# The third norm's rows split in row layout and turned by a transposing DMA in a macaron block

## What is computed

```python
x = x + 0.5 * ffn(layernorm(x), W_up, W_gate, W_down)
x = x + attention(layernorm(x), wq, wk, wv, wo)
x = x + 0.5 * ffn(layernorm(x), W_up, W_gate, W_down)
```

## Time and profile before

| | |
|---|---|
| median of 3 runs | 691.57 us (691.15 to 691.85) |
| the profiled execution | 692.43 us, span of its instructions 690.6 us |
| granted clock of TensorE, mean | 0.973 |
| busy, of the span | PE 603.4 us (87%), ACT 589.8 (85%), DVE 566.4 (82%), POOL 540.2 (78%) |
| DMA queue of the transposes and row copies | 68.1% of 16 engines' time |

### The profile page before, as it was taken

How to read it: one execution, slowest core, us unless ns; L and a number is a source line. 1 busy time by engine, 2 the same in 40 slices (tenths; PEclk the granted TensorE clock), 3 DMA queues, 4 the chain that set the end, 5 groups by cost and what they waited for, 6 DMA issues and landing times. The chain is left out here.

```text
span 690.6 us, 16960 instructions
## 1 busy us (share of the span) xinstructions
PE 603.4 (87%) x5961; PEld 474.4 (69%) x5961; DVE 566.4 (82%) x1457; ACT 589.8 (85%) x1179; POOL 540.2 (78%) x581
## 2 busy tenths in 40 slices
PE   1689996869999999999999999999988887969596
PEld 0366875647878787878787877778775655647374
DVE  3976688878998989898998989989987888777654
ACT  4255589989999999999999999999998999888742
POOL 2045868888989898989898989899897978785533
PEclk9999999999999999999999999999999999897889
DMA  8610419494979585877788696868688989795600
GB/s 328 193 39 1 93 32 196 76 203 77 177 101 189 96 174 110 154 138 129 141 129 164 116 161 119 166 98 169 108 173 144 163 142 182 126 178 92 131 1 32
DMA packets 311573, 90.44 MB, mean 131 GB/s; under 512 B 301760, under 2 KB 310208, under 8 KB 311488
## 3 DMA queue, kind: packets, MB, share of 16 engines
q1 hardware_dynamic: 310624, 87.06, 68.1%
q10 hardware_dynamic: 864, 2.29, 1.0%
HBM read 9.63 MB, written 4.19 MB: 20 GB/s over the span
## 5 line engine op out<-in xcount | busy, mean ns | idle before, releaser
L1614 POOL TENSOR_TENSOR hid_l<-hid,hid_h 128x512 f16<-128x512 f32 x128 | 149.1, 1165 | 91.9 <-ACT hid_h L842 91.8
L823 ACT ACTIVATE prob<-score_ps,exp_bias,exp_scale 128x128 f32<-128x128 f32 (+1 forms) x344 | 149.8, 516 | 9.6 <-DVE exp_bias L1251 8.7
L1609 POOL TENSOR_TENSOR prob_hl<-prob,prob_hl 128x768 f16<-128x768 f32 x86 | 141.9, 1650 | 12.5 <-ACT prob_hl L833 12.3
L416 PE MATMUL down_ps<-tern_down,hid_h 128*128 128x256 f16 x512 | 121.3, 277 | 20.6 <-POOL hid_l L1614 15.3
L416 PE MATMUL down_ps<-tern_down,hid_l 128*128 128x256 f16 x512 | 120.9, 276 | 0.0
L842 ACT ACTIVATE hid_h<-hid 128x512 f16<-128x512 f32 x128 | 81.8, 639 | 38.7 <-DVE hid L1286 38.1
L1277 DVE SCALAR_TENSOR_TENSOR silu_b<-tanh_b,up_ps 128x512 f32<-128x512 f32 x128 | 86.7, 677 | 15.9 <-ACT tanh_b L837 15.8
L837 ACT ACTIVATE tanh_b<-up_ps,tanh_scale 128x512 f32<-128x512 f32 x128 | 89.0, 695 | 12.5 <-PE up_ps L416 12.2
L1241 DVE TENSOR_REDUCE score_ps<-score_ps 128x2 f32<-128x512 f32 x128 | 88.4, 690 | 9.2 <-PE score_ps L426 9.1
L1286 DVE SCALAR_TENSOR_TENSOR hid<-silu_b,gate_ps 128x512 f32<-128x512 f32 x128 | 87.0, 680 | 2.6 <-DVE silu_b L1277 0.3
L424 PE MATMUL score_ps<-mask_b,ident_b 128*128 128x256 bf16 x256 | 69.4, 278 | 16.9 <-ACT prob L823 9.3
(11 more groups left out here) (111 smaller groups left out, 1506.1 us busy)
## 6 DMA issues: line engine op xcount, KB each, us to landing
xs<-x SPq DMA_DIRECT2D x16, 256.0 KB, 2.9
out<-xs SPq DMA_DIRECT2D x16, 256.0 KB, 3.3
raw_w<-prob_hl SPq DMA_TRANSPOSE x86, 3.8
raw_gate<-raw_gate SPq DMA_TRANSPOSE x42, 3.8
raw_up<-w_up_t ACTq DMA_DIRECT2D x1, 512.0 KB, 4.8
raw_gate<-w_gate_t ACTq DMA_DIRECT2D x1, 512.0 KB, 8.1
raw_up<-w_up_t SPq DMA_DIRECT2D x1, 512.0 KB, 9.9
raw_down<-w_down_t ACTq DMA_DIRECT2D x1, 512.0 KB, 10.2
```

What stands on the lines that cost most here:

```text
L416: mm = pe.matmul(dst, lhs, rhs, start=flags and n == 0, stop=n == len(pairs) - 1, skip_group_check=True)
L823: e = act.activation(prob[n % PT_BUFS][:, at + j * width:at + (j + 1) * width], score_ps[:, n % 2 if tile else 2, j * width:(j + 1) * widt ...
L1609: pool.tensor_tensor(prob_hl[n % PT_BUFS][:, 1, :], prob[n % PT_BUFS][:, :], prob_hl[n % PT_BUFS][:, 0, :], ALU.subtract).then_inc(prob_l_ ...
L1614: pool.tensor_tensor(hid_l[:, n % 2, :, :].rearrange("p m n -> p (m n)"), hid[:, n % 2, :], hid_h[:, n % 2, :, :].rearrange("p m n -> p (m ...
```

## The change

The third norm's rows are no longer turned by PE. The root that POOL makes now holds the factor 2^11 that was applied on the way out of PSUM. ACT writes the high part of `xhat` in row layout into a new tile `x_row3`, DVE writes the low part (xhat minus the high part) beside it, and SP issues one transposing DMA of 128x1024 f16 per batch from `x_row3` into the place from which `up` and `gate` read (`turn_xt`, semaphore `xt_turned`). `up` and `gate` of the second block wait for that transfer. The third norm leaves the count of the uses of `misc_ps`. `xt` now describes both layouts; for the third norm the parts lie tile by tile.

Besides, the order within the slots is another for PE, ACT, DVE and POOL, and some of the tables have other values. In the diff this is cut to its core:

```diff
@@ -72,18 +72,18 @@
-SUM_UP_AT = FIRST_FFN - 3
+SUM_UP_AT = FIRST_FFN - 2
...
-POWERS_AT = FIRST_FFN + 2
+POWERS_AT = FIRST_FFN + 1
...
-CASTS_AT = FIRST_FFN + 9
+CASTS_AT = FIRST_FFN + 8
...
-PE_TURN_AT = FIRST_FFN + 1
+PE_TURN_AT = FIRST_FFN + 2
@@ -114,20 +114,26 @@
-    1: {"stats": 4, "mean": 4, "var": 6, "power": 4, "shift": 3, "apply": 3},
-    2: {"stats": 3, "mean": 3, "var": 24, "power": 3, "shift": 2, "apply": 1},
-    3: {"stats": 2, "mean": 1, "var": 26, "power": 2, "shift": 2, "apply": 1},
+    1: {"stats": 5, "mean": 5, "var": 2, "power": 5, "shift": 4, "apply": 2, "turn": 1},
+    2: {"stats": 3, "mean": 3, "var": 11, "power": 3, "shift": 2, "apply": 1, "turn": 0},
+    3: {"stats": 2, "mean": 1, "var": 45, "power": 2, "shift": 2, "apply": 1, "turn": 2},
...
-ROPE_ADD = {-7: 0, -6: 1}
+ROPE_ADD = {-7: 0, -5: 1}
...
+TURNED = (3,)
+MISC_INDEX = {(what, b): n for n, (what, b) in enumerate(
+    (what, b) for _, _, what, b in MISC if not (what.startswith("norm") and int(what[-1]) in TURNED))}
@@ -239,12 +245,17 @@
         rstd = {k: sb(f"rstd{k}", [P, NT]) for k in (1, 2, 3)}
         shift = {k: sb(f"shift{k}", [P, NT]) for k in (1, 2, 3)}
         xhat = {k: sb(f"xhat{k}", [P, NT, E]) for k in (1, 2, 3)}
-        xt_hi = {k: sb(f"xt_hi{k}", [P, XT_BUFS[k], NC, SEQ], F16) for k in (1, 2)}
-        xt_lo = {k: sb(f"xt_lo{k}", [P, XT_BUFS[k], NC, SEQ], F16) for k in (1, 2)}
-
-
-        xt_3 = raw_up[:, :].bitcast(F16)[:, 0:2 * XT_BUFS[3] * NC * SEQ].rearrange("p (a b c n) -> p a b c n", a=2, c=NC, n=SEQ)
-        xt_hi[3], xt_lo[3] = xt_3[:, 0, :, :, :], xt_3[:, 1, :, :, :]
+        x_row = {k: sb(f"x_row{k}", [P, NT, 2, E], F16) for k in TURNED}
+        xt_all = {k: sb(f"xt{k}", [P, XT_BUFS[k] * 2 * W], F16)[:, :] for k in (1, 2)}
+        xt_all[3] = raw_up[:, :].bitcast(F16)[:, 0:XT_BUFS[3] * 2 * W]
+
+        def xt(k, b):
+
+            rows = xt_all[k][:, b % XT_BUFS[k] * 2 * W:(b % XT_BUFS[k] + 1) * 2 * W]
+            if k in TURNED:
+                return rows.rearrange("p (n a c q) -> p a c n q", a=2, c=NC, q=P)
+            return rows.rearrange("p (a c n q) -> p a c n q", a=2, c=NC, q=P)
+
 
         tanh_b = sb("tanh_b", [P, 2, 512])
         silu_b = sb("silu_b", [P, 512])
@@ -318,6 +329,7 @@
         shift_done = {k: sem(f"shift_done{k}") for k in (1, 2, 3)}
         xhat_done = {k: sem(f"xhat_done{k}") for k in (1, 2, 3)}
         xt_hi_done = {k: sem(f"xt_hi_done{k}") for k in (1, 2, 3)}
+        xt_lo_done, xt_turned = ({k: sem(f"{what}{k}") for k in TURNED} for what in ("xt_lo_done", "xt_turned"))
         tanh_done, silu_done, hid_done = sem("tanh_done"), sem("silu_done"), sem("hid_done")
...
@@ -381,6 +393,16 @@
                 sp.dma_start_transpose(k_pad[:, b % 2, :, cols],
                                        k_row[:, tile, :, :].rearrange("p h c -> p (h c)")).then_inc(stk_loaded[tile], 16)
 
+            def turn_xt(k, b):
+
+                if k in TURNED:
+                    if b >= XT_BUFS[k]:
+                        sp.wait_ge(up_done, ROUNDS * added(1 + k // 2, b - XT_BUFS[k]))
+                        sp.wait_ge(gate_done, ROUNDS * added(1 + k // 2, b - XT_BUFS[k]))
+                    sp.wait_ge(xt_lo_done[k], b + 1)
+                    sp.dma_start_transpose(xt_all[k][:, b % XT_BUFS[k] * 2 * W:(b % XT_BUFS[k] + 1) * 2 * W].rearrange("p (m q) -> p m q", q=P),
+                                           x_row[k][:, :, :, :].rearrange("p n a e -> p (n a e)")).then_inc(xt_turned[k], 16)
+
             def turn_probs(n):
 
                 sp.wait_ge(prob_l_done, n + 1)
...
@@ -399,10 +421,12 @@
             def slot(g):
                 if g in FFN_ADD:
                     store(*FFN_ADD[g])
-                for n in pair_of(g, 1):
-                    turn_probs(n)
                 for b, tile in events(g, ROW_LO):
                     turn_rows(b, tile)
+                for n in pair_of(g, 0):
+                    turn_probs(n)
+                for k, b in norms(g, "turn"):
+                    turn_xt(k, b)
@@ -471,13 +495,18 @@
             def up(n, f, b, r):
                 if n < ROUNDS:
                     pe.wait_ge(tern_done[0], n + 1)
-                pe.wait_ge(misc_taken, through(f"norm{2 * f - 1}", b))
+                if 2 * f - 1 in TURNED:
+                    pe.wait_ge(xt_turned[2 * f - 1], 16 * (b + 1))
+                else:
+                    pe.wait_ge(misc_taken, through(f"norm{2 * f - 1}", b))
...
+                if r == 0 and 2 * f - 1 in TURNED:
+                    pe.wait_ge(xt_turned[2 * f - 1], 16 * (b + 1))
...
@@ -513,7 +542,8 @@
             def misc(name, b):
-
+                if name.startswith("norm") and int(name[-1]) in TURNED:
+                    return
...
@@ -785,7 +813,15 @@
-                    split_misc(name, b, xt_hi[k][:, b % XT_BUFS[k], :, :], X_SCALE, xt_hi_done[k])
+                    if k in TURNED:
+                        act.wait_ge(xhat_done[k], b + 1)
+                        if b:
+                            act.wait_ge(xt_turned[k], 16 * b)
+                        act.activation(x_row[k][:, :, 0, :], xhat[k][:, :, :], ACT.Copy).then_inc(xt_hi_done[k], 1)
+                    else:
+                        act.wait_ge(misc_written, through(name, b))
+                        act.activation(xt(k, b)[:, 0, :, :, :].rearrange("p c n q -> p (c n q)"), misc_ps[:, :], ACT.Copy,
+                                       scale=X_SCALE).then_inc(xt_hi_done[k], 1)
...
@@ -844,6 +880,8 @@
             def norm_apply(k, b):
                 act.wait_ge(shift_done[k], b + 1)
+                if k in TURNED and b:
+                    act.wait_ge(xt_lo_done[k], b)
...
@@ -1209,7 +1247,14 @@
-                    low_part(b, xt_lo[k][:, b % XT_BUFS[k], :, :], xt_hi[k][:, b % XT_BUFS[k], :, :], X_SCALE, xt_hi_done[k])
+                    dve.wait_ge(xt_hi_done[k], b + 1)
+                    if k in TURNED:
+                        dve.tensor_tensor(x_row[k][:, :, 1, :], xhat[k][:, :, :], x_row[k][:, :, 0, :], ALU.subtract
+                                          ).then_inc(xt_lo_done[k], 1)
...
@@ -1570,7 +1615,8 @@
-                pool.tensor_scalar(var_s[k][:, :, None], mv[k][:, :, 1:2], LN_EPS, None, ALU.add).then_inc(var_done[k], 1)
+                pool.tensor_scalar(var_s[k][:, :, None], mv[k][:, :, 1:2], LN_EPS,
+                                   X_SCALE ** -2 if k in TURNED else 1.0, ALU.add, ALU.mult).then_inc(var_done[k], 1)
```

1082 lines of the change are left out of this document (542 added, 540 removed).

## The result

| | before | after |
|---|---|---|
| median of 4 runs each, side by side, us | 691.36 (690.16 to 691.85) | 709.68 (706.51 to 712.95) |
| ratio, 95% interval | | 1.0265 (1.0234 to 1.0295) |
| profiled execution, us (span) | 692.43 (690.6) | 709.95 (707.9) |

The prediction said 689.6 us, with a range of 684 to 696. It was wrong in sign and far outside its range.

The account below looks back on a forecast made before the run. It took the full stretch (200 to 500 us) as having no engine with room: PE busy 296.69 of 300 us, ACT 293.77. Terms summed to -2.0 us from the profiled 692.43, giving 690.4, or 689.6 us as median; range 684 to 696.

Parts of the forecast that it names:

- PE's relief (-3.8 us): Full stretch: four norm transposes fewer on PE give back 0.4 us a batch (bounds 0 and 0.48) for 9.5 batches.
- The second rival: Nothing moves: ACT truly bounds the full stretch, PE's relief is worth 0.1 us a batch; 691.4 us, chance 0.20.
- The queue of misc_ps (-2.4 us): Late stretch: transposes leaving the shared PSUM bank's queue free the scores sooner, 0.6 us a batch (0 to 1.0), 4 batches.
- High part on ACT (about 0): Reading the high part from SBUF, not PSUM, costs ACT +0.04 us a batch, 0.6 us in all at most.
- Lock and landing (+2.0 us): DVE's low part and POOL excluding each other, plus PE waiting at gate for the transfer: 0.14 us for 14 batches.
- POOL's order (-1.0 us): With hid_l ahead of the third norm's power, POOL's wait for the mean shrinks: 0.1 us for 9.5 batches (0 to -4).
- Set-up (+1.0 us): Before the first score: powers ahead of silu delay it 2.1 us, to about 35.3; range -2 to +2.1.
- Tail (+2.2 us, 1 to 4): Last two batches: the longer row path is unhidden, up later by +1.4 to +2.0 and +2.1 to +2.5 us.
- All slots of all engines in a new order (4 us both ways): Effects of reordering beyond the priced places, not priceable from rows; allowed 4 us either way.
- rival (1): Row path becomes a wait: gate and up wait for turned rows, low part for POOL; 696 to 700 us, chance 0.33.
- its milder price: Landing only 0.3 to 0.5 us a batch behind PE, giving 692 to 695 us.
- The sign for being wrong: Gate waiting for the transfer over 0.5 us a batch, or ACT's full-stretch busy share being already all there was.

Follow-up runs that it names:

- eighth experiment: Kernel before, with one of norm 3's four PE transposes done instead of four, ACT's and DVE's work kept in size: 694.26 us, ratio 1.0051.
- eleventh: Kernel before's orders, norm 3 by rows and transfer made at the end of slot 0 for batches 0 to 9 only, later ones on PE: 694.15 us.
- fifth experiment: Kernel before's orders with the row path, high and low part of batches 0 to 14 moved to the end of slot 0: 702.17 us, ratio 1.0165.
- ninth experiment: Kernel before, norm 3's low part on DVE reading xhat (SBUF) in place of misc_ps (PSUM), no transfer: 707.35 us, ratio 1.0242.
- twelfth experiment: Kernel before plus 16 transposing DMAs of unread data, the second block's up also waiting for its batch's transfer to land: 708.22 us, ratio 1.0247.
- thirteenth experiment: Changed kernel, up and gate of the second block in batches 1 to 13 reading the previous batch's rows, already landed: 704.42 us, ratio 1.02.
- fourth experiment: Kernel before, with the changed orders and tables before slot 0 only and norm 3 on PE: 690.33 us, ratio 0.9994.
- fourteenth: Changed kernel up to slot 95, rows for batches 0 to 9; from slot 96 orders of before, later batches' norm 3 on PE: 695.72 us, ratio 1.0077.
- eighteenth experiment: Changed kernel up to slot 87, rows for batches 0 to 8; from slot 88 orders of before and norm 3 on PE: 698.90 us, ratio 1.0118.
- the second: Kernel before's orders and tables on PE, ACT, DVE and POOL, with norm 3's row path and transfer added: 728.24 us, ratio 1.0519.
- the third: Changed kernel up to slot 95; from slot 96 the slot orders of before, row path and transfer kept throughout: 709.91 us, ratio 1.028.
- the seventh: Kernel before, norm 3 still on PE, plus 16 same-size DMA transposes on SP that nobody reads or waits for: 688.88 us, ratio 0.9984.

## Why the prediction was wrong, by its own steps

**PE's relief (-3.8 us): worth 0, a step that failed.** The bounds were 0 and 0.48 a batch and the text took 0.4. The eighth experiment gives 396.7 us against 396.6 over the whole full stretch, the eleventh a loss. The argument "ACT has 0.75 us a batch idle, so the larger part can come back" took idle time for room. In the fifth experiment ACT got a wait of 0.45 us a batch for DVE's result, and the batch grew by 0.4. So PE's 98.9% was busy time beside what sets the 36.4 us. That this is a chain through ACT, DVE and POOL is likely by these rows and not shown. The second rival had the worth of the relief right.

**The queue of misc_ps (-2.4 us): not seen.** No kernel that took these transposes off in the late stretch was shorter there: 132.3 to 142.9 us with rows and 136.7 in the eighth experiment, against 132.1.

**High part on ACT (about 0): right.** 630 ns against 598.

**Lock and landing (+2.0 us): the step that failed most.** Its parts were read well: a lock of 0 to 0.9 us (1.25 us in the orders of before; in the changed kernel 10 of the 16 low parts took 0.66 to 0.69 us, the others 0.98 to 1.71), a landing of 3.2 us (2.7 in the median), a wait of 0 to 1 us at gate. Then it took 0.14 us for each of 14 batches, by the slack that DVE and POOL have in sum. The ninth and twelfth experiments show the price of such parts: 1.25 us on DVE cost 12.8 us in the 11 batches up to slot 88, 1.16 a batch; and in the twelfth PE waited 0.73 us in each of 7 batches for a landing that cost 0.5 us a batch. Little was made good. In the changed kernel itself the landing measured 5.3 us without the last two batches (thirteenth experiment). The lock is nearly gone there in the full stretch: its order puts the low part beside a small POOL instruction (rstd), and 8 of the 9 low parts before slot 88 took 0.68 or 0.69 us. The step also looked at the first of two ends only: PE's wait at gate is 2.0 us from 200 to 500 us, but up and tanh of that round are late by the whole way of the rows; 2.5 of tanh's 4.4 us and 2.8 of silu's 11.2 go with the landing.

**The landing in the late stretch** was not priced apart. The thirteenth experiment puts it at 5.1 us of 8.1, by one trace each. The first feed-forward block has ended there, and less other work stands between the low part and gate. PE's waits for the rows are 2.04 us in one batch (at 535.3 us) and 0.32 or 0.33 in three. One of the short ones:

```profile
565.13 0.63 ACT L820 ACTIVATE x_row<-xhat 128x512 f16<-128x512 f32 x1
565.95 0.98 DVE L1252 TENSOR_TENSOR x_row<-xhat,x_row 128x512 f16<-128x512 f32 x1
567.01 1.24 SPq L403 DMA_TRANSPOSE raw_up<-x_row  x1
...
569.79 1.78 PE L440 MATMUL gate_ps<-raw_up,tern_gate 128*128 128x256 f16 x8 [0.33 <-DMA raw_up<-x_row]
...
571.36 1.92 PE L440 MATMUL up_ps<-raw_up,tern_up 128*128 128x256 f16 x8
573.31 0.69 ACT L873 ACTIVATE tanh_b<-up_ps,tanh_scale 128x512 f32<-128x512 f32 x1 [2.24 <-PE up_ps L440]
574.03 0.69 DVE L1322 SCALAR_TENSOR_TENSOR silu_b<-tanh_b,up_ps 128x512 f32<-128x512 f32 x1 [2.59 <-ACT tanh_b L873]
```

PE's own wait is 0.33 us, and the round is late by much more: gate runs first, and eight matmuls take 1.8 to 1.9 us and not 1.0. The granted clock was 1.00 from 560 to 568 us and 0.50 from 570 to 572, the lower of its two levels, after PE had been busy for 4.6 of those 8 us. ACT and DVE then wait 2.2 and 2.6 us. From 520 to 621 us these two waits come to 7.0 and 7.8 us; with the landing taken away (thirteenth experiment, same window) they come to 2.2 and 3.0.

**POOL's order (-1.0 us): the wait went, the gain didn't.** The wait for mv is 2.6 us from 200 to 500 us, against 9.3 before; POOL now waits for hid_h instead, 17.0 us against 10.0, of which 13.5 in the first slot of the batches. That wait stays at 13.2 with the landing taken away, so it is the order's.

**Set-up (+1.0 us): wrong in its reading, small in effect.** The powers come sooner, not later, and silu of the second round starts at 33.88 (33.18 before) and not at 35.3:

```profile
32.77 0.16 DVE L1186 TENSOR_SCALAR w_max<-score_ps 128x4 f32<-128x4 f32 x1 [0.68 <-PE score_ps L769]
...
33.70 0.14 DVE L1201 TENSOR_SCALAR exp_scale<-scale_prod 128x1 f32<-128x1 f32 x1
33.88 0.69 DVE L1322 SCALAR_TENSOR_TENSOR silu_b<-tanh_b,up_ps 128x512 f32<-128x512 f32 x1
```

Against the earlier trace rows, w_max stands 1.7 us sooner. The fourth experiment shows that nothing of it is left at the end.

**Tail (+2.2 us, 1 to 4): measured 7.6 to 7.8.** About half of it, 4.0 us, has come up before batch 14's xhat, where the prediction looked for nothing. Behind it the path was named rightly. From the last batch's xhat to its up it took 5.2 us against 3.2, so the forecast +2.1 to +2.5 was near. For batch 14 it took 7.5 against 3.8, and of that path's three delays only the transfer was priced.

```profile
665.64 0.63 ACT L820 ACTIVATE x_row<-xhat 128x512 f16<-128x512 f32 x1
...
667.79 0.18 DVE L1302 RECIPROCAL inv_sum<-pv_ps 128x4 f32<-128x4 f32 x1 [2.81 <-PE pv_ps L490]
667.89 0.66 DVE L1252 TENSOR_TENSOR x_row<-xhat,x_row 128x512 f16<-128x512 f32 x1
...
671.40 1.89 PE L440 MATMUL gate_ps<-raw_up,tern_gate 128*128 128x256 f16 x8 [1.07 <-DMA raw_up<-x_row]
...
673.09 1.91 PE L440 MATMUL up_ps<-raw_up,tern_up 128*128 128x256 f16 x8
675.04 0.69 ACT L873 ACTIVATE tanh_b<-up_ps,tanh_scale 128x512 f32<-128x512 f32 x1 [8.77 <-PE up_ps L440]
```

High is done at 666.27, but DVE's order has the inverse of an attention product ahead of the low part, and that product waits for its probabilities: 1.6 us. The landing then takes until 671.4, gate stands ahead of up, and both run at the low clock (0.50 granted from 668 to 675 us; PE had been busy for 1.5 of the 8 us before 668). ACT idles for 8.77 us. The last batch has its low part against hid_l on POOL (1.23 us) and up waits 1.45 us for the rows.

**All slots of all engines in a new order (4 us both ways): far too narrow.** The new order saves 18.5 us with the row path and costs 36.5 with the old one. What came was rival (1) in its mechanism and beyond its far end of 700 us: in the full stretch its milder price was met (0.43 us a batch, against 0.3 to 0.5), but the late stretch lost 2.0 a batch and the end nearly 8.

Of the signs named ahead: PE's busy time fell (by 8.4 us, more than the 4 named), the period did not (36.2 to 36.7 us in the quiet batches, 37.4 to 38.2 in three; forecast 36.0); PE's wait for the rows went above 0.3 us (up to 0.67 from 200 to 500 us); the mean of the low part was 0.89 and not 1.1 us; POOL's wait for mv stayed below 5, met; silu at 35.3, missed; the last batch's up came 1.9 us later after xhat, near the 2.3. The sign for being wrong, gate waiting for over 0.5 us a batch, was met in one batch of the full stretch and one of the late one: it was the wrong place to look, as PE's wait is the small end of the delay.

Where the 18 us went: the full stretch lost 4.7 us, of which the landing is 1.8 by the cuts. The late stretch lost 7 to 8, of which the landing is 5.1. The end lost nearly 8. Turning the last batches by PE and going back to the order of before brings the late stretch and the end back together (fourteenth and eighteenth experiment), and 13 of the 18 us by the medians; at the end either half alone keeps the loss. In the orders of before, starting the rows sooner in batch 14 and turning the last two by PE gave half of it each (80.3 to 76.1 to 73.4). The set-up, the transfers' load and PE's relief stand at nothing.

What stays open: whether the waits for turned probabilities are the 3 us that the changed kernel loses in the full stretch with its landing taken away, and which part of the new order makes them; and why the late stretch grows in the eighth experiment when PE has less to do.

## What to carry to other kernels

Before pricing relief on the busiest engine, take the work away and look at the period: 98.9% busy can be worth nothing. When a step is moved from an engine to a DMA, count the way from its input to the first instruction that the next engine needs, not the receiving engine's wait, and start the transfer as early as its input allows (in the orders of before an earlier place of high and low part was worth 26 us), above all where little runs beside it. A new order is no neutral frame for a new path: run each alone, and don't add the two up. And when a DVE instruction gets its last PSUM operand replaced by SBUF, assume that it will end behind the POOL instruction that it meets, or put it where POOL has only small work.

## What the runs showed of the hardware

- A DVE instruction with two SBUF inputs (128x512) that starts during a POOL instruction of 128x512 or 128x768 does not end sooner than 0.54 us behind it: 1.92 us in the ninth experiment's full stretch, where the one with a PSUM input took 0.67 beside the same POOL instruction. With no POOL instruction beside it, or when it started first, it took 0.66 to 0.69 us, so the operand's memory itself costs nothing. One that started during POOL's rstd (128x2) took 0.69 too.
- It works the other way as well. In the changed kernel rstd took 0.70 us when it started ahead of the low part, and 1.18 to 1.21 when it started 0.05 to 0.08 us behind it; raw_gate of 128x768 took 2.10 us instead of 1.64 beside the long low part at 238.28.
- A DMA transpose of 128x1024 f16 inside SBUF lands 2.7 us after its issue (median of 16 in the changed kernel, the second, the third and the twelfth experiment; single ones up to 4.4). At other places it took longer, 3.2 in the fifth and 4.3 in the seventh; q_stk, of the same size, had 3.2 and has 3.7 in the changed kernel. Sixteen of them as mere load changed nothing that can be measured at a DMA share of 0.8. For a transfer issued by GpSimd, the page "DMA: Bandwidth & Descriptors" of the Trainium skill, section "Anatomy of one DMA — SWDGE (gpsimd) path", puts about 2.0 us down as fixed. These are issued by SP, and no run here separates such a part.
- In the late stretch and at the end, eight matmuls behind idle time of PE took 1.8 to 1.9 us instead of 1.04, at a granted clock of 0.50. So a wait that is itself short, 0.33 us, stands in front of a round that is 0.8 us longer for each of its two products.
